# An attention and expert kernel whose first expert's first two tiles are loaded and multiplied ahead of the routing of the last rows

## What is computed

```python
x = x + _L0_xattn_ref(_layernorm(x), ctx_2048, ...)    # theta/phi/g projections, softmax, norm, relu, out_w
x = x + _L0_ffn_ref(_layernorm(x), gate_w, w_gate, w_up, w_down)

# inside _L0_ffn_ref, for the rows xt (2048 x 512)
top_w, top_idx = jax.lax.top_k(softmax(xt @ gate_w.T), 8)
g = silu(einsum('th,ehi->eti', xt, w_gate));  u = einsum('th,ehi->eti', xt, w_up)
y = einsum('eti,eih->eth', g * u, w_down)
out = einsum('eth,te->th', y, full_w)                  # full_w: the 8 weights, normed to 1
```

## Time and profile before

| | |
|---|---|
| median of 3 runs | 759.28 us (755.08 to 759.33) |
| span of the profiled execution | 758.7 us |
| busy: TensorE, VectorE, ScalarE, GpSimd | 708.8, 566.7, 434.8, 380.1 us |
| share of TensorE | 93% |
| moved by DMA | 179.85 MB, 237 GB/s in the mean |
| mean granted TensorE clock | 0.984 |

### The profile page before, as it was taken

How to read it: one execution, slowest core, us unless ns; L and a number is a source line. 1 busy time by engine, 2 the same in 40 slices (tenths; PEclk the granted TensorE clock), 3 DMA queues, 4 the chain that set the end, 5 groups by cost and what they waited for, 6 DMA issues and landing times.

```text
span 758.7 us, 24265 instructions
## 1 busy us (share of the span) xinstructions
PE 708.8 (93%) x3682; PEld 584.4 (77%) x3683; DVE 566.7 (75%) x1355; ACT 434.8 (57%) x1047; POOL 380.1 (50%) x297
## 2 busy tenths in 40 slices
PE   7999999988788799999999999999999999999994
PEld 5466555656667688889988999889988889888993
DVE  4578888878655488677877878877887778767882
ACT  1775666662035366556666666666667566656662
POOL 2006777767776434443544544434553455444554
PEclk9999999999799999999999999999999999999997
DMA  8996777587898999999999999999999999999995
GB/s 297 361 335 234 261 269 288 215 289 273 291 299 188 184 211 224 218 202 237 215 225 240 225 211 238 224 251 228 244 236 245 211 229 248 243 210 227 220 155 79
DMA packets 174405, 179.85 MB, mean 237 GB/s; under 512 B 36864, under 2 KB 128768, under 8 KB 174368
## 3 DMA queue, kind: packets, MB, share of 16 engines
q0 software_dynamic: 30976, 73.48, 43.0%
q1 hardware_dynamic: 118240, 67.67, 35.1%
q10 hardware_dynamic: 25152, 38.30, 15.6%
HBM read 92.25 MB, written 87.13 MB: 236 GB/s over the span
## 4 chain that ended last, share of the span: by engine, by line
SPq 38%; PE 23%; issue 18%; DMA 7%; POOL 7%; ACT 4%; DVE 2%; ACTq 1%; DVEq 1%; POOLq 0%
SPq L320 23%; SPq L325 8%; POOL x_sorted L512 6%; SPq L439 5%; PE bank L1532 3%; PE bank L1533 3%; PE bank L1539 3%; DMA x_sorted<-xn_kept,slots 3%; DMA x_all<-x_sorted 2%; PE bank L1325 2%; DMA x_sorted<-prob,last_slots 1%; PE bank L1504 1%; ACT prob L670 1%; PE bank L1505 1%; PE bank L1506 1%
## 5 line engine op out<-in xcount | busy, mean ns | idle before, releaser
L569 POOL DMA_INDIRECT out_dram<-ctx_all,x_all x144 | 243.2, 1689 | 276.7 <-issue 131.5
L1532 PE MATMUL bank<-gu_hi,xT_hi 128*128 x576 | 194.7, 338 | 2.1 <-ACT xT_hi L800 1.2
L1533 PE MATMUL bank<-gu_lo,xT_hi 128*128 x576 | 195.6, 340 | 0.0
L813 ACT ACTIVATE ctx_all<-bank 128x512 f32<-128x512 f32 x144 | 86.0, 597 | 104.9 <-issue 78.9
L512 POOL DMA_INDIRECT x_sorted<-xn_kept,slots x96 | 100.0, 1042 | 86.7 <-issue 82.0
L1539 PE MATMUL bank<-gu_hi,xT_lo 128*128 x576 | 137.9, 361 | 0.0
L1208 DVE STREAM_TRANSPOSE x_all<-x_all 128x512 f32<-128x512 f32 x146 | 103.9, 712 | 26.5 <-DMA x_all<-x_sorted 22.2
L1255 DVE SCALAR_TENSOR_TENSOR probT<-probT,x_all,bank 128x192 f32<-128x192 f32 x144 | 59.5, 413 | 79.3 <-ACT probT L821 70.5
L1532 PEld LDWEIGHTS bank<-gu_hi,xT_hi 128*128 128x128 f32 x576 | 108.5, 188 | 10.7 <-issue 5.0
L1533 PEld LDWEIGHTS bank<-gu_lo,xT_hi 128*128 128x128 f32 x576 | 108.4, 188 | 5.6
L800 ACT ACTIVATE xT_hi<-x_all 128x512 fp32r<-128x512 f32 x146 | 91.7, 628 | 34.7 <-DVE x_all L1208 34.6
(11 more groups left out here) (222 smaller groups left out, 1109.7 us busy)
## 6 DMA issues: line engine op xcount, KB each, us to landing
x_all<-x_sorted SPq DMA_DIRECT2D x578, 64.0 KB
gu_raw<-in_w_gate_up_dram ACTq DMA_DIRECT2D x28, 768.0 KB
down_raw<-in_w_down_dram ACTq DMA_DIRECT2D x28, 512.0 KB
x_sorted<-pad_rows SPq DMA_DIRECT2D x1, 8720.0 KB, 31.3
x_all<-in_x_dram SPq DMA_DIRECT2D x8, 512.0 KB, 4.9
ctx_all<-in_ctx_dram SPq DMA_DIRECT2D x8, 512.0 KB, 6.6
out_dram<-x_all SPq DMA_DIRECT2D x8, 512.0 KB, 5.9
gu_raw<-in_w_gate_up_dram SPq DMA_DIRECT2D x4, 768.0 KB
```

Of the source, the lines that this page charges most:

```text
L569: pool.indirect_dma_start(out=out, out_offset=bass.IndirectOffsetOnAxis(ap=xw[:, k, E:E + 1].bitcast(I32), axis=0), in_=y_sb[:, i, :], in_ ...
L813: act_e.activation(y_sb[:, i, :], bank[6 + i % 2][:], ACT.Copy).then_inc(S["y_evac"], 1)
L1532: pe.matmul(out_gu, xT_hi[:, s, c * P:(c + 1) * P], gate_up(gu_hi, c), start=(c == 0), stop=False)
L1533: pe.matmul(out_gu, xT_hi[:, s, c * P:(c + 1) * P], gate_up(gu_lo, c), start=False, stop=False)
```

## The change

- Expert 0's tiles are now laid from the region's start: `first_row[0]` is set to its `rowbase`, and it gets at least 2 tiles (`least_tiles`). Its last tile can then reach past its last row, so its whole region is padded: `pad_first_region(b)` writes 256 rows, eight times, and the scatters of batch b wait for it.
- Tiles 0 and 1 (FIXED = 2) then have rows that are known from the start. SyncE loads them behind store 6, once batches 0 to 4 have been scattered and landed and the count of expert 0 in them is at least 256; if it is less, once column 7 of all batches has landed. Store 7 and `load_early(3)` stand behind this in SyncE's queue.
- TensorE, ScalarE and VectorE do tiles 0 and 1 between the making of the tables, and no longer after it, in place of most of `keep_clock`. The small matmuls use other banks.
- LATE goes from 6, 6 to 7, 7: two scatters of batch 6 stand in front of column 7 of batch 7, and two more move behind it. SHARED becomes tiles 2 and 3.
- The first two adds need no test for a new expert.

```diff
-    WARM, WARM_OUT, WARM_FIRST = 20, 10, (28, 38, 10)
-    SHARED = 3
+    WARM, WARM_OUT, WARM_FIRST = 20, 10, 12
+    SHARED = 2, 3
+    FIXED = 2
-    LATE = 6, 6
+    LATE = 7, 7
...
+            def pad_first_region(b):
+
+                if type(b) is not int or b > 0:
+                    sp.wait_ge(S["first_region_padded"], 16 * b)
+                sp.dma_start(x_sorted[bass.ds(P + U * P * b, U * P), :].rearrange("(u p) h -> p u h", p=P),
+                             pad_rows[:].rearrange("p (a h) -> p a h", a=1).to_broadcast([P, U, RW])).then_inc(S["first_region_padded"], 16)
...
             sp.wait_ge(S["const_ready"], 7)
+            pad_first_region(0)
...
                 load_batch(b)
                 store_rows(b - 4)
+                pad_first_region(b - 3)
...
             load_early(2)
-            with sp.Fori(NB - 2, NB) as b:
-                store_rows(b)
+            store_rows(NB - 2)
+            pad_first_region(NB - 1)
+
+            found_need, need_fixed = (sp.alloc_register(n) for n in ("found_need", "need_fixed"))
+            for u in range(U):
+                sp.wait_ge(S[f"scattered{u}"], 16 * TOPK * (NB - 3))
+            sp.wait_ge(S["rows_stored"], 16 * (NB - 1))
+            sp.wait_ge(S["xn2_ready"], U * (NB - 2))
+            sp.wait_ge(S["fixed_rows"], 1)
+            sp.reg_load(found_need, fixed_need[0:1, 0:1])
+            sp.reg_alu(need_fixed, found_need, 1, ALU.max)
+            sp.wait_ge(S["fixed_rows"], sp.snap(need_fixed, min_val=1, max_val=2))
+            for k in range(FIXED):
+                load_x_part(sp, fixed_rows(k), k, range(HC))
+                load_xw(sp, fixed_rows(k), k, k)
+
+            store_rows(NB - 1)
             load_early(3)
...
             sp.wait_ge(last_scattered[TOPK - 1], column_count(TOPK - 1))
-            load_tile(0, 0)
             sp.wait_ge(S["early_ready"], 1)
-            for k in range(1, EARLY):
+            for k in range(FIXED, EARLY):
                 load_tile(0, k)
...
             for k in reversed(range(1, TOPK)):
                 scatter_last(k)
+                if k == TOPK - 3:
+                    for u in range(U):
+                        pool.wait_ge(S[f"scattered{u}"], 16 * (TOPK * (NB - 1) - LATE[u]))
                 if k < TOPK - 2:
                     column_landed(k + 2)
+                if k == TOPK - 3:
+                    pool.sem_inc(S["fixed_rows"], 1)
...
+            transpose_x(0, 0)
             dve.wait_ge(S["cum_done"], 1)
...
+            xT_lo_part(0, 0)
+            transpose_x(0, 1)
+            xT_lo_part(1, 1)
+            gate_product(0, 0, xw[:, 0, 0:1])
             dve.tensor_scalar(is_first, tile_in, 0.0, None, ALU.is_equal).then_inc(S["due_found"], 1)
...
+            for k in range(FIXED):
+                ffn(0, k)
+            keep_clock(WARM_FIRST)
             pe.wait_ge(S["turns_ready"], 3)
```

More of the change, by code:

```diff
@@ L277, in run_tiles @@
             turns = load_turns(eng)
-            for k in range(SLOTS):
+            for k in range(FIXED, SLOTS):
                 step(0, k)
@@ L436, in read_row @@
             def read_row(eight, k):
-                if is_before(eight, k, 1) or not is_before(eight, k, EARLY):
+                if not is_before(eight, k, EARLY):
                     sp.reg_load(row_reg, x_row[0:1, bass.ds(SLOTS * eight + k, 1)])
@@ L727, in load_shared @@
             def load_shared(k):
[L729 to L751 removed]
+                row = early_row(act_e, k, "act_passed", row_reg, code_reg, column_reg, need_reg)
+                load_x_part(act_e, x_sorted[bass.ds(row, P), :], k, range(HC // 2, HC))
             due_reg, gu_due_reg, down_due_reg, gu_raw_due_reg, down_raw_due_reg = (
@@ L835, in _ @@
             act_e.reg_mov(down_raw_reg, 4)
-            for k in range(2):
+            for k in range(FIXED):
                 xT_hi_part(k, k)
+            gate(0, 0)
+            act_e.wait_ge(S["turns_ready"], 3)
+            turns = load_turns(act_e)
+            last = load_last_turn(act_e)
+            act_e.wait_ge(S["pad_zeroed"], 32)
+            for u in range(U):
+                act_e.wait_ge(S[f"scattered{u}"], 16 * (TOPK * (NB - 1) - LATE[u]))
+            act_e.wait_ge(last_scattered[TOPK - 1], column_count(TOPK - 1))
+            act_e.wait_ge(S["rows_stored"], 16 * (NB + 1))
+            act_e.wait_ge(S["early_ready"], 1)
+            for k in SHARED:
+                load_shared(k)
+            split_act_hi(0, 0)
+            gate(1, 1)
+            xT_hi_part(2, 0)
+            xT_hi_part(3, 1)
             act_e.wait_ge(S["tables_ready"], 1)
@@ L1266, in _ @@
             dve.reg_mov(down_done_reg, 2)
-            transpose_x(0, 0)
-            xT_lo_part(0, 0)
-            transpose_x(0, 1)
-            xT_lo_part(1, 1)
+            split_act_lo(0, 0)
+            gate_product(1, 1, xw[:, 1, 0:1])
+            for k in range(2, 4):
+                transpose_x(0, k)
+                xT_lo_part(k, k % 2)
             run_quarters(dve, turns, ffn)
@@ L1542, in ffn @@
                     down(j - 2, (k - 2) % 4, is_before(eight, k, 4))
-            for to, value in ((experts_reg[0], 1), (half_reg[0], 0)):
-                pe.reg_mov(to, value)
+            for k in range(FIXED):
+                pe.reg_mov(experts_reg[k], 1)
+                pe.reg_mov(half_reg[k], 0)
+            pe.wait_ge(S["past_ready"], 2)
+            pe.wait_ge(S["first_row_ready"], 2)
+            pe.matmul(bank[0][0:1, 0:NTX], first_row[:], owned[:], start=True, stop=False)
+            pe.matmul(bank[0][0:1, 0:NTX], spare_col[:], past[:], start=False, stop=True).then_inc(S["row_done"], 1)
+            pe.wait_ge(S["cum_ready"], 3)
+            pe.matmul(bank[1][0:1, 0:NTX], ones_col[:], past[:], start=True, stop=True)
+            pe.matmul(bank[1][0:1, NTX:2 * NTX], n_tile[:], past[:], start=True, stop=True).then_inc(S["owner_done"], 1)
+            for k in range(FIXED):
+                ffn(0, k)
+            keep_clock(WARM_FIRST)
             pe.wait_ge(S["turns_ready"], 3)
```

158 lines of the change are left out of this document (73 added, 85 removed).

## The result

| | before | after |
|---|---|---|
| median of the runs (20 each, us) | 758.45 | 766.0 |
| lowest to highest (us) | 755.08 to 764.53 | 759.21 to 770.71 |
| profiled execution: span (us), clock | 758.7, 0.984 | 759.3, 0.976 |
| DMA traffic | 179.85 MB at 237 GB/s | 184.28 MB at 243 GB/s |

The ratio after to before is 1.0087, with a 95% interval of 1.0065 to 1.0110: the change costs 4.9 to 8.3 us, with 6.6 as the middle. I had forecast 758.8 us and a range up to 761.5; the measured median is above it.

The account below looks back on a forecast made before the run. The prediction took saturated GpSimd, scattering column 0 ahead of tile 10's load, as the wall, with TensorE the bound from tile 10 on. 0 - 0.5 + 0.2 + 0.3 = 0.0 against 758.7; forecast 758.8 us, range 754.3 to 761.5.

Parts of the forecast that it names:

- The wall: Saturated GpSimd scatters column 0 last, at 236.36; tile 10's load waits for it until 242.98: change of the end 0.
- Rival R1: Tile 10's load not tied to GpSimd's instructions, so the 4.2 us lead reaches the end: 754.5 us; chance 0.12.
- R3: Expert 0 has fewer than 256 rows, so tiles 0 and 1 load after column 7: 758.7 us; chance 0.01.
- The two adds stand where they stood: GpSimd's queue before column 0: still 32 scatters and 2 adds, so column 0 is issued at 236.36 as before.
- The pads, "charged at 0": Padding DMAs of expert 0's region, about 2.0 us each of all DMA engines: hidden, as GpSimd sets the pace.
- R2: Pads delay scatter landings `keep_rows` awaits in batch steps 3 to 7: up to 2.0 us each, 772.7 us; chance 0.07.
- The order of the late scatters, "0": LATE from 6 to 7 only reorders GpSimd's scatters; their number before column 0 stays 32: cost 0.
- Tile 2: Takes tile 1's place, held by the column count: first matmul at 212.55 instead of 216.75, 4.2 us sooner.
- The wait of TensorE, foreseen as 9 to 11 us: After tile 9's matmuls with hi parts, TensorE waits 9 to 11 us where it now waits 4.51.
- (a) Landing: Column 0's last scatter to release: shorter without tile 9's load in the queue, 0 to -2.7 us, taken as -0.5.
- (b) Clock: TensorE's granted clock at half rate again after the longer wait: 0 to +1.5 us, taken as +0.2.
- (c) The port: VectorE's subtractions of tiles 0 and 1 lengthen other GpSimd scatters: 0 to +2.4 us, taken as +0.3.

Follow-up runs that it names:

- e1: The kernel after, but the second add no longer waits for the first add to land: 763.92 us, ratio 1.0041 to before.
- e6: The kernel after without the second add's wait and with two pads for eight: 759.93 us, ratio 1.0015 to before.
- e8: The kernel after without the second add's wait and with tiles up to 13 loaded early: 752.74 us, ratio 0.9908 to before.
- e7: The kernel before with tiles 2 to 13, not only 2 to 9, loaded early: 756.47 us, ratio 0.9977 to before.
- e2: The kernel before with only the unconditional wait ahead of the first two adds: 763.31 us, ratio 1.0038 to before.
- e4: The kernel after with two pads for eight, the second add's wait kept: 764.81 us, ratio 1.0061 to before.
- e3: The kernel before with only the eight pads and the scatters' waits for them: 760.3 us, ratio 1.0008 to before.
- e5: The kernel after once more, unaltered, on another chip: 765.11 us, ratio 1.0072 to before.
- e9: The kernel before with the eight pads and the wait ahead of the first two adds, in a slower call: ratio 1.0114 to before.
- e18: The kernel after, wait kept, with column 0's last scatter ahead of the second add, in a slower call: ratio 1.0065 to before.
- e17: The kernel before with the eight pads and the wait ahead of the first two adds, in a slower call: ratio 1.0050 to before.

## Why the prediction failed, step by step

**The wall: right at the seam.** Column 0 to tile 10's load to TensorE at the product of tile 8 is the chain that decides when TensorE goes on. In eight kernels (before, after, e1 to e6) it does so 8.6 to 9.5 us behind tile 10's load, which stands anywhere from 242.98 to 252.69. e8 cuts the chain and gains, on one chip; e7 cuts it and meets another wait. Rival R1, the lead passing through, didn't come: tile 10's load came later and not sooner. R3 fell too: tiles 0 and 1 were loaded at 178.49 and 182.06, as placed.

**"The two adds stand where they stood": the step that failed.** Their place is the same, but not what they wait for. In before the first two adds test whether a new expert begins and pass; in after they call the wait without the test. My text on the change had it as a test fewer, a saving, and I never asked what stands behind the test. The wait costs 4.7 us on the engine that I had just called saturated, between the last work that is ready and column 0. In the time it is 3.5 us (after less e1) or 2.9 (e2 alone).

**The pads, "charged at 0": mis-sized.** They cost 2.3 us of GpSimd's chain. In the time it is about 2 (e1 less e6, and after less e4, each 2.0, each from two calls and for six of the pads), but only 0.6 (-1.6 to 2.8) where they stand alone, in e3. I had weighed only one way in which a pad can be felt, the landing that `keep_rows` waits for, and found it covered. That one isn't seen; most of the gaps are released by VectorE's slots, and the scatters themselves are a little longer. Load 4 did go out 1.6 us later, as I had allowed for, and it is not the cause (e4 and e6). R2 named these pads as the slower rival at 2.0 us apiece; it came to 2.3 us for all eight. The sign I had given for it, gaps of over 0.3 us between 62 and 166 and batch 5 later than 169.1, is what after shows (81.93, 125.24; 170.79).

**The order of the late scatters, "0": 0.8 us off.** Their number is the same, but column 7 now follows two scatters sooner, and VectorE's `last_slots` isn't there: the 1.09 us at 197.50. A reordering of a queue can meet inputs that the old order covered.

**Tile 2: near.** Tile 0's first matmul was placed at 199 and came at 200.92; tile 2's at 212 and came at 214.78. I had let it hang on the column count, but SyncE's half of its load went at 205.19, so the count was there by then. ScalarE issued the halves of tiles 2 and 3 from 207.53 to 210.44, and only then, at 210.48, rounded the hidden values of an early tile, behind which VectorE's transpose of tile 2 stands in order (213.16). Why ScalarE's issue came at 207.53 isn't shown. The wait of TensorE, foreseen as 9 to 11 us, was 12.84.

**The corrections.** (a) Landing: right, and larger, -1.8 us within the 0 to -2.7 that I gave. The other kernels bear out the cause, how closely tile 9's load goes ahead of the last scatter: with 0.05 and 3.7 us between the two (e3, before) the landing takes 6.82 and 6.62 us up to tile 10's load, with 6.5 and 7.2 us (e2, e6) 5.09 and 5.83, with 10.8 and more (e1, after, e4, e5) 4.83 to 4.98. In before 0.7 us of it is the last scatter's own length, 1.62 for 0.96. (b) Clock: +0.5 for +0.2. (c) The port: nothing more than in before. The scatter of 3.40 us at 190.44 is the one at 188.06 of before. GpSimd's groups of after, which answer to the earlier trace rows:

```profile
L544 POOL DMA_INDIRECT x_sorted<-prob,last_slots x16 | 16.1, 1006 | 5.7 <-issue 4.0 <-DVE last_slots L927 1.1 <-DMA x_sorted<-prob,last_slots 0.6
L544 POOL DMA_INDIRECT x_sorted<-late_rows,late_slots x16 | 15.9, 995 | 4.9 <-issue 4.9
```

1006 and 995 ns against 1028 and 1035: in the mean the scatters didn't get slower. Single ones did, in both kernels. These are scatters and subtractions of after:

```profile
202.23 0.66 DVE L1198 TENSOR_TENSOR xT_lo<-x_all,xT_hi 128x512 fp32r<-128x512 f32 x1
202.57 1.17 POOL L544 DMA_INDIRECT x_sorted<-prob,last_slots  x1 [0.30 <-issue]
204.04 0.96 POOL L544 DMA_INDIRECT x_sorted<-prob,last_slots  x1 [0.30 <-DMA x_sorted<-prob,last_slots]
204.21 0.69 DVE L1198 TENSOR_TENSOR xT_lo<-x_all,xT_hi 128x512 fp32r<-128x512 f32 x1 [0.70 <-ACT xT_hi L823]
219.61 0.69 DVE L1198 TENSOR_TENSOR xT_lo<-x_all,xT_hi 128x512 fp32r<-128x512 f32 x1
219.68 1.45 POOL L544 DMA_INDIRECT x_sorted<-prob,last_slots  x1 [0.30 <-issue]
```

A scatter that begins inside a subtraction of VectorE ends some 0.8 us after it, as the one at 190.44 does after the second of the two long ones (191.78, 1.22 us); a subtraction that begins inside a scatter (204.21) takes its usual 0.69 us, and so does the scatter its 0.96. Among the 32 scatters after has three of the first kind (1.17, 1.40 and 1.45 us) and before four (1.29, 1.47, 1.28 and 1.62). The Trainium skill (SBUF — State Buffer, "SBUF: two separate sides") speaks of a port pair that VectorE and GpSimd share and that whoever starts first holds. The trace agrees where VectorE starts first and not where GpSimd does.

**The sum as it should have been**, at the seam of the profile: 2.4 (the stretch starts later) + 0.8 + 4.7 - 0.3 = 7.6 for column 0, -1.8 for the landing, -0.8 from the load to TensorE (8.69 us against 9.49), +0.5 for the clock = 5.5 us. The runs have 6.6 with an interval of 4.9 to 8.3. That these terms are the whole is argued, not shown: the wait and the pads alone, in before, were measured together only in the slower calls of e9 to e18. But e6, which has neither the wait nor most of the pads, is left with +1.1 (-1.5 to 3.7), which needs no further cause.

## What to carry to other kernels

When a change makes a condition constant, look at what it guarded: a test that always fell through may have been hiding a wait, and a wait in a queue that is saturated costs its whole length to everything behind it. Ask of each wait whose landing it is and how long ago that was issued; in e18's trace four independent scatters between the two cover it. And an early start is worth its time only if the next release doesn't hang on the queue that has become the bound: two tiles ahead gave nothing in front of column 0, and 7 us on one chip once tile 10 no longer waited for it. The same edit gave nothing clear in the slower calls, and in e7 it met the next wait, so look behind the wall for what comes next before you pay for moving it.

## What the runs showed of the hardware

- GpSimd, waiting for an accumulating scatter to `out_dram` to land, is released 6.3 to 6.7 us after the start of its issue: in after the second add starts 6.62 us behind the first, in e2 6.66 us, in e5 6.34. In the slower calls it was 5.67 us in e9 and 6.19 in e17.
- The profile names ScalarE as the releaser of the second add in after, e4 and e5, and the DMA in e2; e1 shows that in after it was the DMA. For e4 and e5 that follows only from the same code and the like length (4.70 and 4.39 us). In e1 the second add goes at once behind the first, so ScalarE's rows were there.
- After 12.84 us without work TensorE's granted clock stayed at 0.50 for 4.5 us of work, after 4.51 us without work for 3.5 us.
- In before and after, a 128-row scatter that began inside a two-input subtraction of VectorE took 1.17 to 1.62 us (3.4 beside two long ones) where most take 0.96; a subtraction that began inside a scatter took its usual 0.69 us (204.21 in after).
- From the issue of column 0's last scatter to tile 10's load it was 6.82 us with tile 9's load issued 0.05 us ahead of that scatter (e3), and 4.83 to 4.98 with 10.8 us or more between them.
- In three calls the kernel before took 75 to 95 us longer. In the ten profiles of these calls the granted clock from 60 to 260 us is 0.78 to 0.90, where before has 1.00 and 0.93, with waits whose releaser the records don't name. Its cause is open.
